# Attention preparation hosted in the feed-forward block ahead of it and in the score loop, with fp32r shift turns, on one Trainium2 core

## The chip, the cores and the metric

The kernel runs on one core of one Trainium2 (trn2) chip. The metric is the device time of one execution in microseconds (us), lower is better. TensorE (PE) multiplies, VectorE (DVE), ScalarE (ACT) and GpSimd (POOL) work on tiles, and SyncE (SP) issues most DMAs.

## What is computed

The reference carries x, 4 x 256 tokens of 256 features, through six residual stages. The change touches the borders of the fifth, an attention with ALiBi bias and low-rank keys and values:

```python
x = x + 0.5 * _L0_ffn_ref(_layernorm(x), ...)      # dense plus 2 of 8 experts, GELU
x = x + _L0_attn_ref(_layernorm(x), ...)
x = x + 0.5 * _L0_ffn_ref(_layernorm(x), ...)
x = x + 0.5 * _L1_ffn_ref(_layernorm(x), ...)      # 4 of 8 experts, ReLU
x = x + _L1_attn_ref(_layernorm(x), ...)
x = x + 0.5 * _L1_ffn_ref(_layernorm(x), ...)

# _L1_attn_ref, 16 heads of 16
c_kv = hidden_states @ w_dkv.T                     # 128 columns
q = (hidden_states @ w_q.T).reshape(B, S, HEADS, HEAD_DIM)
k = (c_kv @ w_uk.T).reshape(B, S, HEADS, HEAD_DIM)
v = (c_kv @ w_uv.T).reshape(B, S, HEADS, HEAD_DIM)
scores = jnp.einsum('bqhd,bkhd->bhqk', q, k) * scale + alibi_bias(S)[None, None]
attn = jax.nn.softmax(scores, axis=-1)
out = jnp.einsum('bhqk,bkhd->bqhd', attn, v).reshape(B, S, HIDDEN)
return out @ w_o.T
```

## The kernel before

The 1024 tokens are two blocks of 512 (`BLK`), and every stage goes over both, block 0 and then block 1. Each engine has its own program, written out by hand; semaphores tie them. Matrices are multiplied as three fp32r products: a value is split into a high part (rounded by ScalarE, names ending in `_hi`) and a low part (value minus high part, by VectorE or GpSimd, `_lo`), and `split3` (lines 578 to 581) issues high by high, high by low and low by high.

**The block ahead.** The ReLU feed-forward (`ffn1`) has 8 units, one per expert. Unit n: upper half (lines 731 to 734, into PSUM bank n % 3), relu twice on ScalarE (lines 1118, 1119), low part on GpSimd (line 523), lower half (`down1`, line 740) two units later (`LAG`), and the accumulate into x on VectorE (`acc1`, line 1579). The routing chain (logits, top 4, exponentials by ScalarE in `exps`, weights) must end before unit 0 is accumulated, and `down1` of unit n waits for the accumulate of unit n - 2. Its block 1 also carries the rounding of the attention weights (`wa_h` on ScalarE at unit 2, `wa_l` in four pieces on GpSimd at units 4 to 7), the constant rows of the key stacks (unit 4), and the statistics and normalisation of the attention's block 0 (units 4 and 5, `prepare_at`).

**The attention.** `attn1` on TensorE (line 753) turns z of block 0 (in `block_start`), finishes the last two units, and then projects c, q in two halves of 8 heads and k in two halves for block 0, turns z of block 1, projects v in two halves, and c and the first half of q of block 1. SyncE writes each half of q and k, high and low parts, to DRAM (`write`) and reads them back stacked by head (`read`: three DMAs into `qs`, six into `ks`), 96 rows of 32 that make the three products one. Four stack parts of 8 heads are in SBUF at a time.

**The loop.** 78 steps, one per head (64 heads) and a tail. At step s: `scores(s)`; at step s >= 7 `scores_t(s - 7)`, the turned scores whose exponential ScalarE takes; every fourth step a `shift_turn`, and from step 14 on every fourth a `pv`. VectorE adds the bias to each score and keeps the row minimum (`bias_min`, line 1662), which `shift_hi` and `shift_lo` split into columns of `shift`. `shift_turn` (line 862) turns four 128-column tiles of `shift` through `pe.transpose` with the f32 identity, and ScalarE copies the result to rows 96 to 127 of the query stack. The missing projections of block 1 (k half 0, q half 1, k half 1) stand at steps 1, 3 and 5:

```python
for s in range(4 * HEADS + SUM):
    if s < 4 * HEADS:
        scores(s)
    if s == 1:
        project_k(1, 0)
    if s == 3:
        project_q(1, 1)
    if s == 5:
        project_k(1, 1)
    if TURN <= s < 4 * HEADS + TURN:
        scores_t(s - TURN)
```

## Time and profile before

| | |
|---|---|
| median of 3 runs | 534.08 us (532.31 to 534.1) |
| the profiled execution's own time | 532.84 us |
| its span in the profile | 531.1 us |
| mean granted TensorE clock | 0.982 of 2.4 GHz |
| busy: PE, DVE, ACT, POOL | 497.2, 384.8, 252.4, 109.6 us |

The span is what the profile shows of one execution; the execution's own time has a little around it. In the profile PE is the matrix products, PEld their weight loads, which run beside them. A product's record begins when it starts and ends when its result is out, so that records overlap: the distance between two starts is what one costs. A line number is that of the kernel before. `x8` behind a row says that it merges eight instructions, and the bracket gives the idle time before it and who ended it.

### The profile page before, as it was taken

The numbers are of one execution on the slowest core, as the hardware profiler recorded it, in microseconds if no ns is written. First come the engines' busy times: TensorE is split into PE (matmuls) and PEld (weight loads), VectorE is DVE, ScalarE is ACT, GpSimd is POOL, SyncE is SP. The second block draws the span as 40 slices with busy tenths as digits, with TensorE's granted clock in tenths as the row PEclk, the third lists the DMA queues.
The fourth block names the chain that finished last, engine by engine and source line by source line (L and its number), as shares of the span: only waits on it lengthen the run. The fifth ranks groups of instructions, "written<-read, shape, count | busy, mean of one in ns | idle before, by whom it ended". The sixth has DMA issues, their size and how long they took to land.

```text
span 531.1 us, 9082 instructions
## 1 busy us (share of the span) xinstructions
PE 497.2 (94%) x3074; PEld 422.9 (80%) x3074; DVE 384.8 (72%) x1196; ACT 252.4 (48%) x539; POOL 109.6 (21%) x170
## 2 busy tenths in 40 slices
PE   2999999999999999999999997899789989799996
PEld 1788888888888888888888886788667878678885
DVE  4669787674687674688588787878767878648776
ACT  3657643525323525324574237456445766644441
POOL 1001000110010110010002005637403333414352
PEclk9999999999999999999999999899997999899999
DMA  6432320000000000001200000276488430000011
GB/s 206 118 90 68 97 56 1 1 1 1 2 0 1 1 1 1 1 1 41 60 21 0 2 1 2 91 81 118 150 187 269 111 79 3 1 2 1 3 38 41
DMA packets 18797, 25.87 MB, mean 49 GB/s; under 512 B 2848, under 2 KB 12832, under 8 KB 18752
## 3 DMA queue, kind: packets, MB, share of 16 engines
q1 hardware_dynamic: 17696, 24.78, 17.8%
q10 hardware_dynamic: 1056, 0.51, 0.3%
q8 instruction: 25, 0.41, 0.3%
q14 instruction: 20, 0.16, 0.1%
HBM read 17.42 MB, written 5.24 MB: 43 GB/s over the span
## 4 chain that ended last, share of the span: by engine, by line
PE 79%; DVE 9%; issue 4%; ACT 3%; POOL 2%; SPq 2%; DMA 1%; DVEq 0%; ACTq 0%; POOLq 0%
PE ps L579 22%; PE ps L581 21%; PE ps L580 21%; DVE x L1590 3%; PE ps L908 2%; PE ps L860 2%; PE ps L594 2%; PE ps L891 2%; PE ps L981 1%; DVE ps L1673 1%; POOL al L523 1%; PE ps L872 1%; PE ps L889 1%; ACT z L1013 1%; PE ps L970 1%
## 5 line engine op out<-in xcount | busy, mean ns | idle before, releaser
L579 PE MATMUL ps<-zh,w0u_h 128*128 128x512 f32 x256 | 103.1, 403 | 1.5 <-ACT zh L1020 1.5
L581 PE MATMUL ps<-zl,w0u_h 128*128 128x512 f32 x256 | 102.3, 400 | 0.0
L580 PE MATMUL ps<-zh,w0u_l 128*128 128x512 f32 x256 | 102.1, 399 | 0.0
L1042 ACT ACTIVATE gel<-ps 128x512 f32<-128x512 f32 x64 | 38.2, 597 | 104.4 <-PE ps L581 104.3
L1408 DVE TENSOR_TENSOR act<-gel,ps 128x512 f32<-128x512 f32 x64 | 43.7, 683 | 42.4 <-ACT gel L1042 42.2
L579 PE MATMUL ps<-w0d_h,ah 128*128 128x256 f32 x256 | 73.0, 285 | 0.4
L581 PE MATMUL ps<-w0d_l,ah 128*128 128x256 f32 x256 | 71.5, 279 | 0.0
L580 PE MATMUL ps<-w0d_h,al 128*128 128x256 f32 x256 | 71.4, 279 | 0.0
L1048 ACT ACTIVATE ah<-act 128x512 fp32r<-128x512 f32 x64 | 40.2, 629 | 40.3 <-DVE act L1408 40.3
L1590 DVE SCALAR_TENSOR_TENSOR x<-ps,aff,x 128x256 f32<-128x256 f32 x128 | 53.0, 476 | 8.9 <-PE ps L581 7.1
L579 PEld LDWEIGHTS ps<-zh,w0u_h 128*128 128x128 f32 x256 | 48.7, 190 | 12.8 <-ACT zh L1020 1.8
L523 POOL TENSOR_TENSOR al<-act,ah 128x512 fp32r<-128x512 f32 x32 | 42.0, 1313 | 79.1 <-ACT ah L1119 75.8
L1415 DVE TENSOR_TENSOR al<-act,ah 128x512 fp32r<-128x512 f32 x64 | 43.8, 684 | 19.9 <-ACT ah L1048 19.6
L581 PEld LDWEIGHTS ps<-zl,w0u_h 128*128 128x128 f32 x256 | 48.6, 190 | 11.8
L580 PEld LDWEIGHTS ps<-zh,w0u_l 128*128 128x128 f32 x256 | 48.7, 190 | 9.6
L579 PEld LDWEIGHTS ps<-w0d_h,ah 128*128 128x128 f32 x256 | 48.0, 188 | 3.7 <-issue 1.4
L580 PEld LDWEIGHTS ps<-w0d_h,al 128*128 128x128 f32 x256 | 48.0, 188 | 2.2
L1673 DVE CUSTOM_DVE_ANT_0 ps<-ps,bias 128x256 f32<-128x256 f32 (+1 forms) x128 | 42.5, 384 | 9.1 <-PE ps L860 8.3
L581 PEld LDWEIGHTS ps<-w0d_l,ah 128*128 128x128 f32 x256 | 48.0, 188 | 0.0
L1390 DVE SCALAR_TENSOR_TENSOR macc<-ps,aff,macc 128x256 f32<-128x256 f32 x112 | 46.3, 475 | 0.4
L579 PE MATMUL ps<-w_h,ah 128*128 128x256 f32 x128 | 36.8, 287 | 3.8 <-DVE x L1590 3.4
L500 POOL TENSOR_SCALAR ssq_e<-ssq 128x4 f32<-128x4 f32 x12 | 2.3, 193 | 184.4 <-ACT sq L1027 184.3
(182 smaller groups left out, 1039.7 us busy)
## 6 DMA issues: line engine op xcount, KB each, us to landing
stage<-in_w_dram SPq DMA_DIRECT2D x16, 384.0 KB, 3.0
qs<-split_out SPq DMA_DIRECT2D x24, 128.0 KB, 3.0
ks<-split_out SPq DMA_DIRECT2D x48, 64.0 KB, 2.9
stage<-in_w_dram SPq DMA_DIRECT2D x8, 256.0 KB, 2.7
ks<-pad SPq DMA_DIRECT2D x6, 256.0 KB, 9.7
ks<-pad SPq DMA_DIRECT2D x1, 1024.0 KB, 8.8
split_out<-qh SPq DMA_DIRECT2D x4, 256.0 KB, 2.6
split_out<-ql SPq DMA_DIRECT2D x4, 256.0 KB, 3.0
```

The lines of the kernel that those rows point to most:

```text
L523: nc.gpsimd.tensor_tensor(al[:, slot, :], act32[:, n % 2, :], ah[:, slot, :].bitcast(F32), ALU.subtract).then_inc(al1_s, 1)
L579: pe.matmul(o, lh, rh, start=start, stop=False, **kw)
L580: pe.matmul(o, ll, rh, start=False, stop=False, **kw)
L581: return pe.matmul(o, lh, rl, start=False, stop=stop, **kw)
L594: mm = pe.transpose(ps[:, kc, t * P:(t + 1) * P], z2[:, NORMS[p][1], t, kc * P:(kc + 1) * P], ident[:, :])
L1042: nc.scalar.activation(gel[:, n % 2, :], ps[:, 2 * (n % 2), :], ACT.Gelu_apprx_tanh).then_inc(gelu_s, 1)
L1048: nc.scalar.activation(ah[:, n % NA, :], act32[:, n % 2, :], ACT.Copy).then_inc(ah_s, 1)
L1390: i = V.scalar_tensor_tensor(sums[:, t, :], o, a, sums[:, t, :], ALU.mult, ALU.add)
L1408: V.tensor_tensor(act32[:, n % 2, :], gel[:, n % 2, :], ps[:, 2 * (n % 2) + 1, :], ALU.mult)\
L1415: V.tensor_tensor(al[:, n % NA, :], act32[:, n % 2, :], ah[:, n % NA, :].bitcast(F32), ALU.subtract)\
L1590: i = V.scalar_tensor_tensor(xt, ps[:, base + t // 2, (t % 2) * D:(t % 2 + 1) * D], aff[:, b, t, e:e + 1], xt, ALU.mult, ALU.add)
L1673: i = V.tensor_tensor_reduce(s, s, bias[:, cols], 1.0, FAR, ALU.add, ALU.min, nmin[:, hd // GROUP % 2, c, j:j + 1])
```

## The change

It moves preparation, and it changes how the shift columns are turned.

- **Block 0** of the attention is prepared inside block 1 of the feed-forward ahead of it, which it calls the host (`hosts_attn1`). VectorE takes the statistics at unit 1 ahead of the routing, GpSimd scales there, ScalarE normalises at unit 2. TensorE turns z after the upper half of unit 4, and projects c at unit 5, q at units 5 and 6, k at units 6 and 7. The attention weights are rounded at unit 0 (low parts at units 0 to 3), the constant rows at unit 1. Their loads start when the last lower half of the GELU feed-forward is done. The upper halves of the host go through two PSUM banks instead of three, and z and k of block 0 are split into unused slots of the query stack (`zh2`, `zl2`, `kh[0]`, `kl[0]`).
- **Block 1** is prepared in the loop: v half 1 of block 0 at step 1, z turned at step 8, c and q half 0 at step 11, k half 0 at 14, q half 1 at 17, k half 1 at 20, with ScalarE's and VectorE's parts one step later. The banks and the waits that guard them follow.
- **The queue** reads the first stack before it writes k half 1.
- **The shift columns** of the four tiles of a turn lie 32 columns apart in `pad`, so that the tiles overlap, and a turn is four plain fp32r products with an identity that ScalarE has rounded.

```diff
...
 Z_STEP = 66
+V0_STEP = 1
+Z1_STEP, C1_STEP, K10_STEP, Q11_STEP, K11_STEP = 8, 11, 14, 17, 20
...
         ql = sb("ql", [P, 2, BLK], F32R)
-        kh, kl = ah, al
...
         ks = sb("ks", [P, SLOTS, 2, SEQ], F32R)
+        zh2, zl2 = [qs[:, i:i + 4, :].rearrange("p (c s) q -> p c (s q)", c=KC) for i in (0, 4)]
+        kh, kl = [[qs[:, i:i + 4, :].rearrange("p (m s) q -> p m (s q)", m=2), t] for i, t in ((8, ah), (12, al))]
...
         pbt = sb("pbt", [P, 2, 4, 3 * P])
-        shift = macc[:, :, :].rearrange("p t d -> p (t d)").rearrange("p (s c m) -> p s c m", s=2, c=4)
...
+        ident_r = wr_h[:, 0, 0, :]
+        shift = pad[:, 0:2 * (K_ROWS + P)].rearrange("p (s m) -> p s m", s=2)
+        shift_cols = shift[:, :, K_ROWS:K_ROWS + P].rearrange("p s (c m) -> p s c m", c=4)
...
+        def hosts_attn1(st, b):
+            return st.kind == "ffn1" and st.after == "attn1" and b == 1
...
-            return 5 if b == 0 else 4
+            return 1 if hosts_attn1(st, b) else 5 if b == 0 else 4
...
+        def up_bank(n):
...
+            return n % 2 if "attn1" in stages and n // U1 == blocks_before_attn1 - 1 else n % 3
...
+        def zt_bank(p, kc):
...
+            return {attn1_p: (2, 3), attn1_p + 1: (PV_BANK, OUT_BANK)}.get(p, (0, 1))[kc]
...
+        def split_z(p):
+            return (zh2, zl2) if p == attn1_p else (zh, zl)
...
             if "attn1" in stages:
-                for b in range(2):
-                    sp.wait_ge(x_s[b], last_ffn0 + 1)
+                sp.wait_ge(down_s, U0 * f0)
...
                 sp.wait_ge(zero_s, 6 * 16)
-                for m, kind in ((0, 0), (1, 0), (0, 1), (1, 1)):
+                for m, kind in ((0, 0), (0, 1), (1, 0)):
                     write(0, m, kind)
-                for h in range(4):
+                read(0)
+                write(0, 1, 1)
+                for h in range(1, 4):
...
                         ln_scale(norm(st, b) + 1)
-                    if st.k + b == 1 and c >= U1 - WL and "attn1" in stages:
-                        i = c - (U1 - WL)
+                    if hosts_attn1(st, b) and c < WL:
+                        i = c
...
                     nc.gpsimd.memset(va[:, :, :, HD:HD + 1], 1.0).then_inc(wal_s, 1)
-                    nc.gpsimd.memset(shift[:, :, :, :], 0.0).then_inc(shz_s, 1)
+                    pool.wait_ge(zero_s, 6 * 16)
+                    pool.wait_ge(pad_s, 16)
+                    nc.gpsimd.memset(shift.bitcast(F32), 0.0).then_inc(shz_s, 1)
                     pool.wait_ge(shz_s, 1)
-                    nc.gpsimd.memset(shift[:, :, :, ONE_COL:ONE_COL + 1], 1.0).then_inc(shz_s, 1)
+                    nc.gpsimd.memset(shift_cols[:, :, :, ONE_COL - K_ROWS:ONE_COL - K_ROWS + 1].bitcast(F32), 1.0).then_inc(shz_s, 1)
...
                         if n >= 3:
-                            pe.wait_ge(ah1_s, n - 2)
+                            pe.wait_ge(ah1_s, n - 1 if hosts_attn1(st, b) else n - 2)
                         for kc in range(KC):
-                            mm = split3(ps[:, n % 3, :], w1_h[:, c, kc * P:(kc + 1) * P], w1_l[:, c, kc * P:(kc + 1) * P],
+                            mm = split3(ps[:, up_bank(n), :], w1_h[:, c, kc * P:(kc + 1) * P], w1_l[:, c, kc * P:(kc + 1) * P],
...
                             logits(3, routed["ffn1", fb])
+                        host = hosts_attn1(st, b)
+                        if host and c == 4:
+                            transposes(attn1_p)
+                        if host and c == 5:
+                            pe.wait_ge(wal_s, WL)
+                            split_ready(attn1_p)
+                            project_c(0)
+                        if host and c == 6:
+                            project_k(0, 0)
+                        if host and c == 7:
+                            project_k(0, 1)
...
                             down1(n - LAG)
+                        if host and c == 5:
+                            project_q(0, 0)
+                        if host and c == 6:
+                            project_q(0, 1)
...
                 block_start(st, 0)
-                pe.wait_ge(wal_s, WL)
-                split_ready(p)
-                project_c(0)
-                project_q(0, 0)
-                project_q(0, 1)
-                project_k(0, 0)
+                project_v(0)
                 pe.wait_ge(acc_s, E * f0 + U1 * st.d1 - 1)
-                project_k(0, 1)
-                transposes(p + 1)
-                project_v(0)
-                project_v(1)
-                split_ready(p + 1)
-                project_c(1)
-                project_q(1, 0)
...
                         scores(s)
-                    if s == 1:
-                        project_k(1, 0)
-                    if s == 3:
-                        project_q(1, 1)
-                    if s == 5:
-                        project_k(1, 1)
...
                         project_v(2 + V_STEPS.index(s))
+                    if s == V0_STEP:
+                        project_v(1)
+                    if s == Z1_STEP:
+                        transposes(p + 1)
+                    if s == C1_STEP:
+                        split_ready(p + 1)
+                        project_c(1)
+                        project_q(1, 0)
+                    if s == K10_STEP:
+                        project_k(1, 0)
+                    if s == Q11_STEP:
+                        project_q(1, 1)
+                    if s == K11_STEP:
+                        project_k(1, 1)
...
                 if g == 0:
+                    pe.wait_ge(ident_r_s, 1)
                     pe.wait_ge(shz_s, 2)
-                    pe.wait_ge(ch_s, 2)
-                    pe.wait_ge(cl_s, 2)
+                    pe.wait_ge(v_s, 2)
...
                 for i in range(4):
-                    mm = pe.transpose(ps[:, 2, i * P:(i + 1) * P], shift[:, g % 2, i, :], ident[:, :])
+                    mm = pe.matmul(ps[:, 2, i * P:(i + 1) * P], shift[:, g % 2, SLOT * i:SLOT * i + P], ident_r,
+                                   start=True, stop=True)
...
                             logits_t_out(routed["ffn1", fb], 3)
+                        host = hosts_attn1(st, b)
+                        if host and c == 6:
+                            q_hi(0, 0)
+                        if host and c == 7:
+                            q_hi(0, 1)
...
                             act.wait_ge(ob_ps, 8)
-                        nc.scalar.activation(act32[:, n % 2, :], ps[:, n % 3, :], ACT.Relu)
-                        nc.scalar.activation(ah[:, (U0 * f0 + n) % NA, :], ps[:, n % 3, :], ACT.Relu).then_inc(ah1_s, 1)
+                        nc.scalar.activation(act32[:, n % 2, :], ps[:, up_bank(n), :], ACT.Relu)
+                        nc.scalar.activation(ah[:, (U0 * f0 + n) % NA, :], ps[:, up_bank(n), :], ACT.Relu).then_inc(ah1_s, 1)
+                        if host and c == 4:
+                            z_hi(attn1_p)
+                        if host and c == 5:
+                            c_hi(0)
+                        if host and c in (6, 7):
+                            k_hi(0, c - 6)
...
                             normalise(p + b + 1)
-                        if fb == 1 and c == 2 and "attn1" in stages:
+                        if host and c == 0:
...
                             nc.scalar.activation(wa_h[:, :], wa_raw, ACT.Copy).then_inc(wah_s, 1)
-                        if fb == 1 and c == 4 and "attn1" in stages:
+                        if host and c == 1:
...
                             nc.scalar.activation(pad[K_ROWS:P, :], rows_raw, ACT.Copy).then_inc(rows_s, 1)
+                            nc.scalar.activation(ident_r, ident[:, :], ACT.Copy).then_inc(ident_r_s, 1)
...
                 p = st.p
-                z_hi(p)
-                c_hi(0)
-                q_hi(0, 0)
-                q_hi(0, 1)
-                k_hi(0, 0)
-                k_hi(0, 1)
-                normalise(p + 1)
-                z_hi(p + 1)
                 v_out(0)
-                v_out(1)
-                c_hi(1)
-                q_hi(1, 0)
-                k_hi(1, 0)
-                q_hi(1, 1)
-                k_hi(1, 1)
...
                                 out_hi(n, t)
+                    if s == Z1_STEP - 4:
+                        normalise(p + 1)
...
                         normalise(p + 2)
+                    if s == V0_STEP + 1:
+                        v_out(1)
+                    if s == Z1_STEP + 1:
+                        z_hi(p + 1)
+                    if s == C1_STEP + 1:
+                        c_hi(1)
+                        q_hi(1, 0)
+                    if s == K10_STEP + 1:
+                        k_hi(1, 0)
+                    if s == Q11_STEP + 1:
+                        q_hi(1, 1)
+                    if s == K11_STEP + 1:
+                        k_hi(1, 1)
...
                                 out_lo(3, 1)
+                        host = hosts_attn1(st, b)
...
                             left_acc(st, b, 2 - c)
+                        if host and c == 1:
+                            prepare(attn1_p, 0)
...
                             acc1(n - 3)
+                        if host and c == 4:
+                            z_lo(attn1_p)
+                        if host and c == 5:
+                            c_lo(0)
+                        if host and c in (6, 7):
+                            q_lo(0, c - 6)
+                            k_lo(0, c - 6)
...
                         first = prepare_at(st, b)
-                        if c == first or c == first + 1:
+                        if not host and c in (first, first + 1):
...
                 dve.wait_ge(kh_s, 2 * b + m + 1)
-                if b:
-                    dve.wait_ge(written_s[1][m], 32)
-                V.tensor_tensor(kl[:, m, :], ps[:, k_bank(b, m), :], kh[:, m, :].bitcast(F32), ALU.subtract)\
+                V.tensor_tensor(kl[b][:, m, :], ps[:, k_bank(b, m), :], kh[b][:, m, :].bitcast(F32), ALU.subtract)\
...
                 left_acc(st, 0, 3)
-                z_lo(p)
...
                 prepare(p + 1, 0)
-                c_lo(0)
-                q_lo(0, 0)
-                q_lo(0, 1)
-                k_lo(0, 0)
-                k_lo(0, 1)
-                z_lo(p + 1)
-                c_lo(1)
-                q_lo(1, 0)
...
                         bias_min(s)
-                    if s == 1:
-                        k_lo(1, 0)
...
                         shift_lo(s // GROUP)
-                    if s == 3:
+                    if s == Z1_STEP + 1:
+                        z_lo(p + 1)
+                    if s == C1_STEP + 1:
+                        c_lo(1)
+                        q_lo(1, 0)
+                    if s == K10_STEP + 1:
+                        k_lo(1, 0)
+                    if s == Q11_STEP + 1:
                         q_lo(1, 1)
-                    if s == 5:
+                    if s == K11_STEP + 1:
```

The places in the programs of the engines, as built:

ScalarE in block 1 of the host, from the copy of unit 0's logits (`small`, before) and from the relu of unit 0 (after), to the exponentials of the routing (`lex`). Before:

```order
L1032 ACTIVATE small<-ps 8x512
L1118 ACTIVATE act<-ps 128x512
L1119 ACTIVATE ah<-ps 128x512
L1118 ACTIVATE act<-ps 128x512
L1119 ACTIVATE ah<-ps 128x512
L1118 ACTIVATE act<-ps 128x512
L1119 ACTIVATE ah<-ps 128x512
L1036 ACTIVATE lex<-lsh 128x32
L1130 ACTIVATE wa_h<-va 128x1792
```

and now:

```order
L1158 ACTIVATE act<-ps 128x512
L1159 ACTIVATE ah<-ps 128x512
L1176 ACTIVATE wa_h<-va 128x1792
L1158 ACTIVATE act<-ps 128x512
L1159 ACTIVATE ah<-ps 128x512
L1179 ACTIVATE pad<-pbt 32x512
L1180 ACTIVATE wr_h<-ident 128x128
L1158 ACTIVATE act<-ps 128x512
L1159 ACTIVATE ah<-ps 128x512
L1071 ACTIVATE lex<-lsh 128x32
L1048 ACTIVATE z<-x,shift_z,zs 128x256 x4
```

The weights, the constant rows (`pad`) and the identity (into `wr_h`) stand ahead of `lex`, and the normalisation (`z`) right behind it, ahead of unit 3's relu.

TensorE in the loop, steps 9 to 11 and the scores of step 12. `ks,qs` with 256 columns alone are scores, `qs,ks` pairs are turned scores, `wr_h,pad` is a shift turn, `zh` and `zl` with `wa` are c and q. There was nothing of block 1 at these steps before. Now:

```order
L910 MATMUL ps<-wr_h,pad 128x128 x4
L895 MATMUL ps<-ks,qs 128x256
L898 MATMUL ps<-ks,qs 128x256
L924 MATMUL ps<-qs,ks 128x128
L926 MATMUL ps<-qs,ks 128x256
L898 MATMUL ps<-ks,qs 128x256
L924 MATMUL ps<-qs,ks 128x128
L926 MATMUL ps<-qs,ks 128x256
L603 MATMUL ps<-zh,wa_h 128x512
L604 MATMUL ps<-zh,wa_l 128x512
L605 MATMUL ps<-zl,wa_h 128x512
L603 MATMUL ps<-zh,wa_h 128x512
```

Eight more of the `wa` products follow before the next score.

The SP queue around the first stack read. Before:

```order
L401 DMA split_out<-qh 128x512
L401 DMA split_out<-ql 128x512
L401 DMA split_out<-qh 128x512
L401 DMA split_out<-ql 128x512
L401 DMA split_out<-ah 128x512
L401 DMA split_out<-al 128x512
L401 DMA split_out<-ah 128x512
L401 DMA split_out<-al 128x512
L412 DMA qs<-split_out 32x4x256 x3
L420 DMA ks<-split_out 16x4x256 x6
```

and now:

```order
L422 DMA split_out<-qh 128x512
L422 DMA split_out<-ql 128x512
L422 DMA split_out<-qs 128x512 x2
L422 DMA split_out<-qh 128x512
L422 DMA split_out<-ql 128x512
L433 DMA qs<-split_out 32x4x256 x3
L441 DMA ks<-split_out 16x4x256 x6
L422 DMA split_out<-qs 128x512 x2
```

The last pair of writes, k half 1 (`qs`, where its parts now lie), stands behind the first read.

## Rows read from the trace of the kernel before

**Rows 1.** The page, part 1: busy us (share of the span) xinstructions of each engine.

```profile
PE 497.2 (94%) x3074; PEld 422.9 (80%) x3074; DVE 384.8 (72%) x1196; ACT 252.4 (48%) x539; POOL 109.6 (21%) x170
```

**Rows 2.** Busy time by stretch: us, PE, PEld, DVE, ACT, POOL, PEclk, DMA share, GB/s.

```profile
373.40:390.50 17.10, 13.00 (x59) 10.36 (x57) 9.45 (x24) 8.53 (x15) 4.23 (x8) 0.90 0.60 184
390.50:405.20 14.70, 12.81 (x63) 10.74 (x63) 13.08 (x69) 6.47 (x13) 2.43 (x6) 0.82 0.78 202
405.20:450.00 44.80, 42.36 (x419) 34.27 (x419) 36.62 (x204) 30.67 (x70) 16.94 (x42) 0.98 0.36 100
```

**Rows 3.** The same view, one stretch of 2 us.

```profile
402.00:404.00 2.00, 2.00 (x11) 2.00 (x11) 1.64 (x10) 0.98 (x2) 0.87 (x3) 0.50 0.84 255
```

**Rows 4.** Waits of TensorE, 373 to 412 us: total, times, longest.

```profile
PE ps L594 <- ACT z L1013: 2.6, 1, 2.6
```

**Rows 5.** Timeline of TensorE, feed-forward block 1: start, us, line, operation.

```profile
360.98 0.39 PE L579 MATMUL ps<-zh,w_h 128*128 128x512 f32 x1
...
362.34 0.28 PE L579 MATMUL ps<-w_h,ah 128*128 128x256 f32 x1
...
363.75 0.40 PE L579 MATMUL ps<-zh,w_h 128*128 128x512 f32 x1
```

**Rows 6.** Timeline of VectorE, the same block.

```profile
352.12 0.19 DVE L1328 COPY lg<-ps 128x32 f32<-128x32 f32 x1 [2.33 <-PE ps L609]
...
357.67 3.42 DVE L1590 SCALAR_TENSOR_TENSOR x<-ps,aff,x 128x256 f32<-128x256 f32 x8
```

**Rows 7.** Timeline of ScalarE, the same block.

```profile
354.70 0.23 ACT L1036 ACTIVATE lex<-lsh 128x32 f32<-128x32 f32 x1
354.82 1.71 ACT L1130 ACTIVATE wa_h<-va 128x1792 fp32r<-128x1792 f32 x1
...
364.78 2.08 ACT L1013 ACTIVATE z<-x,shift_z,zs 128x256 f32<-128x256 f32 x4 [1.15 <-POOL shift_z L496]
```

**Rows 8.** Timeline of GpSimd, the same block.

```profile
362.90 0.19 POOL L486 TENSOR_SCALAR zs_e<-mv 128x4 f32<-128x4 f32 x1 [1.08 <-DVE mv L1296]
...
364.70 1.16 POOL L537 TENSOR_TENSOR wa_l<-va,wa_h 128x448 fp32r<-128x448 f32 x1
365.81 1.30 POOL L523 TENSOR_TENSOR al<-act,ah 128x512 fp32r<-128x512 f32 x1
```

**Rows 9.** Timeline of the SP queue, first stack read.

```profile
383.46 1.85 SPq L412 DMA_DIRECT2D qs<-split_out  x3
385.35 2.77 SPq L420 DMA_DIRECT2D ks<-split_out  x6
```

**Rows 10.** Timeline of TensorE, first score, turned score and PV.

```profile
390.50 0.39 PE L857 MATMUL ps<-ks,qs 96*128 96x256 f32 x1 [0.84 <-DMA ks<-split_out]
...
397.17 0.28 PE L889 MATMUL ps<-qs,ks 128*128 128x128 f32 x1
...
405.24 1.08 PE L908 MATMUL ps<-pbt,va 128*32 128x256 f32 x8
```

**Rows 11.** Timeline of VectorE, steps 4 to 8 of the loop.

```profile
394.93 0.69 DVE L1603 SCALAR_TENSOR_TENSOR ql<-ps,qh 128x512 fp32r<-128x512 f32 x1
395.53 0.29 DVE L1673 CUSTOM_DVE_ANT_0 ps<-ps,bias 128x128 f32<-128x128 f32 x1
...
399.24 0.29 DVE L1673 CUSTOM_DVE_ANT_0 ps<-ps,bias 128x128 f32<-128x128 f32 x1
```

**Rows 12.** Timeline of TensorE, a shift turn and what follows.

```profile
415.05 0.60 PE L872 MATMUL ps<-ident,macc 128*128 128x128 f32 x4
415.40 0.36 PE L579 MATMUL ps<-wa_h,ch 128*128 128x256 f32 x1
415.61 0.28 PE L580 MATMUL ps<-wa_h,cl 128*128 128x256 f32 x1
```

**Rows 13.** Timeline of TensorE, an fp32r product of 128 columns.

```profile
407.37 0.22 PE L889 MATMUL ps<-qs,ks 128*128 128x128 f32 x1
407.44 0.33 PE L891 MATMUL ps<-qs,ks 128*128 128x256 f32 x1
```

88 lines of the change are left out of this document (44 added, 44 removed).

## Prediction

> **What bounds the kernel now.** I read the page first: TensorE is busy for 94% of the span of 531.1 us, 497.2 us [rows 1]. So a gain must come from the few places where it waits or runs at a low clock, or from its own work. Then I cut the span into stretches. From 345 us to 373.4 us, the feed-forward block ahead of the attention, TensorE is hardly idle. The projections from there to the first score take 17.1 us at a mean clock of 0.90; the first fourteen steps of the loop take 14.7 us at 0.82; after them TensorE is busy for 42.36 of 44.80 us [rows 2]. In the two slow stretches the clock stands either at 1.00 or at 0.50, that is at 1.2 of 2.4 GHz [rows 3]. The waits say why: TensorE stood 2.6 us for ScalarE's normalised block 1 [rows 4], and its first score began 0.84 us late on a stack read [rows 10]. In the fourteen steps VectorE is busy for 13.08 of 14.70 us [rows 2]: there it is the bound, and TensorE starves beside it. After 405.2 us it is TensorE again.
>
> **The unit prices.** At the full clock the upper half of an expert, six products of 512 columns, takes 1.4 us of TensorE, and the lower half, twelve of 256 columns, takes 1.4 us [rows 5]. By these, c, each half of q, and the two halves of k together are 1.4 us each, one half of k and a v half are 0.7 us. A block's eight turns of z take 0.8 us if I take the 0.09 us per turn that four f32 turns show (0.35 us, 415.05 to 415.40) [rows 12].
>
> **Part A, to the first score.** Block 0's z turns, c, q and k go between units 4 to 7 of the block before. TensorE's work is the same wherever it stands: c, q, k are 5.6 us, and v half 0 is 0.7 us, so 6.3 us of the old stretch remain ahead of the first score. Block 1's turns, c and q half (3.6 us at full clock) and v half 1 (0.7 us) go behind it, and so does the 2.6 us wait. To the 6.3 us come stalls:
> - ScalarE now rounds the attention weights (1.71 us) after unit 0, and the constant rows and the identity (about 0.9 us) after unit 1; all of it stood behind the exponentials of the routing before. They started at 354.70 us [rows 7] and now start at 356.2 us by my walk. VectorE's routing weights wait for them, so the first accumulate slides from 357.67 us [rows 6] to 358.8 us, and TensorE's unit-2 lower half from 359.5 to 360.6 us. The new z turns fill 0.8 us of that; 0.65 us stay idle.
> - VectorE's statistics (1.8 us) move ahead of the routing. They fit in the 2.33 us in which it waited for the logits [rows 6], so I charge nothing; with that cover gone, each us would fall on the same chain.
> - GpSimd's four pieces of the weights' low part (1.16 us each) now alternate with units 0 to 3, with the 1.80 us of the scale between (362.90 to 364.70), and each unit's own low part takes 1.30 us [rows 8]. That is 11.6 us against 11.2 us of TensorE's four units. ScalarE's normalise (2.08 us) [rows 7] stands ahead of unit 3's relu. GpSimd's fourth piece ends at 363.7 us, 0.4 us after TensorE wants it.
> - The last three accumulates queue behind q's and k's low parts on VectorE: 0.6 us.
> - The stack. The SP queue must write q half 0, k half 0 and q half 1, then read: 1.85 us and 2.77 us of issue [rows 9], and 2.4 us from the end of issue (388.12) to the first score (390.50) [rows 10]. q half 1 is split at 374.3 us by my walk, its write is issued at 375.3 us, so the stack is there at 382.4 us; TensorE is ready at about 380.7 us. I take 1.9 us of waiting. The queue's order puts k half 1 behind this read; otherwise it would be 1 us more.
> Two stalls in that block, 0.6 us, are overtaken. So A takes 6.3 + 0.65 + 0.4 + 0.6 + 1.9 - 0.6 = 9.2 us instead of 17.1 us: **7.9 us gained**. Bounds: no new stall, 6.3 us; every stall twice as long, 12.8 us.
>
> **Part B, steps 0 to 14.** Before, 14.7 us, of which 6.7 us to the first turned score (390.50 to 397.17) and 8.1 us to the first PV (405.24) [rows 10]. VectorE needs 3.7 us for four heads (395.53 to 399.24), among it one low part like the one of 0.69 us at 394.93 [rows 11], so 3.0 us without: 0.75 us per step. In steps 0 to 7 nothing of block 1 is left to do but v half 1. I take 5.8 us, less than before by the 0.9 us of low parts that are gone. Steps 7 to 14 are 5.25 us of VectorE; z's, c's and q's low parts are 2.8 us more, and TensorE has 3.6 us (turns, c, q half) that it does in one piece while scores wait. The two do not overlap well, since c waits for z's low part behind two heads: 9.5 us. TensorE starves from 380.7 to 388 us, longer than ahead of the slow clock of before, so I add 2.0 us for half clock. B is then 17.3 us: **2.6 us lost**. Bounds: 14.0 us (VectorE's 10.5 + 2.8 us and a start of 0.7 us, no half clock) and 20.5 us.
>
> **Part C, from step 14.** k half 0, q half 1 and k half 1, once in steps 1 to 5, now stand at steps 14, 17 and 20 where TensorE is the bound: 2.8 us lost. The half clock that ran on to 407 us is over by then: 0.8 us gained. The shift turns: four f32 turns take 0.35 us, and the product behind them takes 0.21 us (415.40 to 415.61) where 256 columns go in 0.12 us: 0.44 us in all [rows 12]. An fp32r product of 128 columns is followed after 0.07 us [rows 13], so four are 0.27 us: 0.17 us less for each of 16 turns, 2.7 us, of which I take **2.0 us** because some lie where TensorE waits anyway. Bounds 0 and 2.7 us. Part C sums to zero. The rounding of the identity has no row: between the 0.23 us of the exponentials [rows 7] and the 1.71 us of the weights; 0.3 us is in the list above. The later clearing of the shift columns on GpSimd ends before the first turn. The earlier weight load moves to a time in which the DMA engines do nothing.
>
> The Trainium skill speaks against the turn: "TensorE: Matmul & The Clock Gate", Terms, says of transpose mode that it is 4x faster for FP32, and the new turn gives that mode up. By it a turn would cost four times as much; an fp32r product of 128 columns runs in 0.07 us without the mode [rows 13], so for this type the trace disagrees, and the sum goes by the row.
>
> **Sum.** 7.9 - 2.6 + 0 = 5.3 us. Against the profiled execution's own 532.84 us that gives **527.5 us**. The median of the three runs is 534.08 us, 1.2 us above it, and the lowest 532.31 us; 0.5% (2.7 us) is about what a measurement of this kernel can tell from no change.
>
> **Rivals.**
> - *The fill hides it all.* Block 1's split runs in VectorE's gaps and the clock stays up, so B takes 14.0 us: 524.2 us. For it: VectorE is idle while TensorE does c and q in one piece. Against: TensorE starves from 380.7 us on, and both drops of the clock in this region came behind such a time.
> - *The host block eats it.* The upper halves go through two PSUM banks there instead of three: unit n now needs the relu of unit n - 2, which sits behind weights, rows and normalise on ScalarE. If the late exponentials, the weights' low part and the stack cost 5 us more than I have, it comes to 532.5 us, no change. For it: ScalarE's row of 1.71 us lands on a chain that TensorE already waited for.
> - *Slower: five stations.* Each preparation step of block 1 (z, c with q, k, q, k) makes TensorE wait for a split on ScalarE and VectorE: 0.5 us of high part (1.71 us for 1792 columns [rows 7], here 512), 0.69 us of low part [rows 11] and a head of 0.75 us ahead of it, 1.9 us in all. It decides if three steps (2.6 us of loop) are less than that round trip with its queues. Stalling in full at all five is 9.5 us, where I have 1.5 us in B: 8 us more, 535.5 us.
> - *Slower: the turn loses its mode.* Four times 0.35 us is 1.40 us, 1.13 us above the 0.27 us that I have, for 16 turns 18 us: 545.5 us. The products of 0.07 us [rows 13] speak against it. This is what the Trainium skill's rule named above would make of the turn.
> - *The turns are not on the path.* Then the 2.0 us are missing: 529.5 us.
>
> **How the numbers follow.** The forecast 0.42, the hidden fill 0.27, turns off the path 0.05, the host block 0.16, five stations 0.08, the lost mode 0.02. The first three are faster by over 0.5%, and some of the host block's cases too: 0.76; within 0.5% 0.14; slower 0.10. The range runs from 521.5 us (the hidden fill with half of A's stalls gone) to 532.5 us (the host block); what is left out are the two slower cases, 0.10, and some 0.1 of the others' tails.
>
> **What would show it.** The first score at about 382.5 us, behind a wait for the stack of some 2 us; the first PV near 400 us; the clock at 0.50 for some 4 us behind the first score. The exponentials of the second block near 356 us. A turn of four products followed after 0.27 us. If the first score comes later than 386 us, part A is wrong; if the waits for VectorE's low parts in steps 9 to 20 sum to over 4 us, the stations are right; if the clock stays at 1.00, the hidden fill is.

## The result, and the profile after

The changed kernel is slower: a median of 536.58 us (12 runs, 533.61 to 537.72) beside 532.33 us (12 runs, 530.2 to 534.12) for the kernel before on the same chip. The ratio is 1.0068, its interval 1.005 to 1.0086. The forecast was 527.5 us. The profiled execution took 536.63 us, with a span of 534.9 us, against 532.84 and 531.1 us before: 3.8 us more, which is what has to be explained.

The page's part 1, after:

```profile
PE 498.6 (93%) x3074; PEld 425.1 (79%) x3074; DVE 386.2 (72%) x1196; ACT 251.6 (47%) x540; POOL 109.4 (20%) x170
```

Against [rows 1] TensorE has 1.4 us more of work and 2.4 us more of idle time. Where they lie shows when the attention is cut at its first score, its first PV product and its last. The timeline of TensorE, first score, the c product of block 1 and the first PV (start, us, line, operation, idle before and what ended it):

```profile
382.24 0.35 PE L895 MATMUL ps<-ks,qs 96*128 96x256 f32 x1 [1.52 <-DMA ks<-split_out]
...
396.40 0.52 PE L603 MATMUL ps<-zh,wa_h 128*128 128x512 f32 x1 [1.30 <-ACT zh L1055]
396.72 0.63 PE L604 MATMUL ps<-zh,wa_l 128*128 128x512 f32 x1
397.15 0.63 PE L605 MATMUL ps<-zl,wa_h 128*128 128x512 f32 x1
...
403.46 0.64 PE L943 MATMUL ps<-pbt,va 128*32 128x256 f32 x8 [0.71 <-DVE cl L1666]
```

The view of busy time, cut at those points (columns as in [rows 2]):

```profile
373.40:382.24 8.84, 6.78 (x50) 6.13 (x49) 6.68 (x17) 2.32 (x5) 3.76 (x5) 1.00 0.86 229
382.24:403.46 21.22, 16.64 (x78) 14.24 (x79) 13.73 (x72) 9.00 (x18) 4.06 (x10) 0.76 0.43 116
403.46:475.00 71.54, 64.04 (x597) 51.80 (x597) 50.69 (x266) 45.95 (x104) 25.04 (x62) 0.95 0.25 75
```

| stretch | before, us | after, us | lost | forecast |
|---|---|---|---|---|
| 373.4 us to the first score | 17.1 | 8.84 | -8.3 | -7.9 |
| first score to first PV | 14.7 | 21.2 | +6.5 | +2.6 |
| first PV to last PV | 66.0 (405.24 to 471.2) | 71.5 (403.46 to 475.0) | +5.5 | 0 |

Behind the last PV both need 59.9 us more. So the host block gave what the forecast said, and 14 steps and the rest of the loop took 12.0 us where the forecast had 2.6 us.

Who stood still there is seen in VectorE's waits, 380 to 425 us (line, waited for: total, times, longest):

```profile
DVE ps L1725 <- PE ps L898: 8.1, 7, 3.3
DVE zl L1364 <- ACT zh L1055: 2.3, 1, 2.3
DVE al L1670 <- ACT ah L1194: 1.7, 2, 1.4
```

VectorE, the bound of the first steps, stands 2.3 us for the rounded z and 1.4 us for the last half of k. The timelines of ScalarE and VectorE show why:

```profile
390.29 0.49 ACT L1256 ACTIVATE pbt<-ps 128x384 f32<-128x384 f32 x1 [0.36 <-PE ps L926]
393.39 0.59 ACT L1249 ACTIVATE qs<-ps 32x512 fp32r<-32x512 f32 x1 [2.60 <-PE ps L910]
394.00 0.49 ACT L1256 ACTIVATE pbt<-ps 128x384 f32<-128x384 f32 x1
394.39 1.08 ACT L1055 ACTIVATE zh<-ps 128x512 fp32r<-128x512 f32 x2
```

```profile
392.56 0.14 DVE L1725 DVE_READ_ACCUMULATOR2_ANT nmin<- 128x1 f32 x1
395.01 1.29 DVE L1364 TENSOR_TENSOR zl<-ps,zh 128x512 fp32r<-128x512 f32 x2 [2.31 <-ACT zh L1055]
...
401.27 0.30 DVE L1725 CUSTOM_DVE_ANT_0 ps<-ps,bias 128x128 f32<-128x128 f32 x1 [3.29 <-PE ps L898]
```

TensorE turned z at step 8 (from 390.06 us). But ScalarE's program has z's high part at step 9, behind that step's copy of the shift rows (L1249), and the copy waits 2.60 us for a shift turn that TensorE does in step 9 too. A turn falls on every fourth step, at 9 and again at 21, and the high part of k half 1 is placed at step 21: the same knot twice. VectorE, which runs in order, cannot pass its own wait; then TensorE has no scores, starts c 1.30 us late, and VectorE in turn waits 3.29 us for TensorE.

The Trainium skill, "TensorE: Matmul & The Clock Gate", Part 1, "Architectural detail: the array is 16× 32×32, not 1× 128×128", says of ScalarE and VectorE that they are strict first-in first-out; by that rule a free z in PSUM is of no use while the copy ahead of it waits, and the trace agrees: 2.60 us.

The clock is the second half of it. Busy time of stretches, after:

```profile
384.00:386.00 2.00, 0.62 (x3) 0.41 (x3) 2.00 (x13) 0.49 (x2) 1.43 (x3) 1.00 0.47 133
394.00:396.00 2.00, 0.48 (x3) 0.30 (x2) 0.99 (x2) 2.00 (x5) 0.49 (x2) 1.00 0.53 161
462.00:464.00 2.00, 0.40 (x4) 0.23 (x3) 1.01 (x6) 2.00 (x6) 0.19 (x1) 1.00 0.00 0
384.00:400.00 16.00, 12.35 (x48) 10.56 (x49) 10.07 (x54) 6.64 (x14) 3.46 (x8) 0.68 0.46 125
416.00:420.00 4.00, 3.20 (x16) 3.20 (x17) 2.36 (x14) 1.34 (x3) 0.82 (x2) 0.65 0.88 261
464.00:468.00 4.00, 3.82 (x24) 3.19 (x28) 0.85 (x2) 2.58 (x7) 1.45 (x4) 0.62 0.02 4
```

The first three rows are times in which TensorE starves, busy for 0.40 to 0.62 of 2.00 us; from 416 to 417 us it is busy for 0.20 of 1.00 us. Behind each of the four the granted clock stood at 0.50, that is 1.2 of 2.4 GHz, for some 3 to 6 us. The products of c above follow each other after 0.43 us, where at the full clock it is 0.23 us [rows 5].

### The profile page after: what moved, and what is told of

It reads as the page before. It is cut to its first block, busy times and chain, and to the rows that moved or that the text cites. A ratio compares the mean times of both kernels' runs of the same rounds, so it can differ in the third digit from the quotient of the medians.

```text
span 534.9 us, 9080 instructions
## 1 busy us (share of the span) xinstructions
PE 498.6 (93%) x3074; PEld 425.1 (79%) x3074; DVE 386.2 (72%) x1196; ACT 251.6 (47%) x540; POOL 109.4 (20%) x170
## 4 chain that ended last, share of the span: by engine, by line
PE 80%; DVE 7%; issue 4%; ACT 4%; POOL 3%; DMA 1%; SPq 0%; DVEq 0%; POOLq 0%; ACTq 0%
PE ps L603 23%; PE ps L605 22%; PE ps L604 22%; DVE x L1648 2%; PE ps L615 2%; PE ps L943 2%; POOL al L545 2%; PE ps L1016 1%; PE ps L898 1%; DVE ps L1725 1%; PE ps L926 1%; ACT z L1048 1%; PE ps L910 1%; PE ps L1005 1%; DMA x<-in_x_dram 1%
## 5 line engine op out<-in xcount | busy, mean ns | idle before, releaser
L605 PE MATMUL ps<-w0d_l,ah 128*128 128x256 f32 x256 | 71.5, 279 | 0.0
L1256 ACT ACTIVATE pbt<-ps 128x384 f32<-128x384 f32 x64 | 30.8, 494 | 19.8 <-PE ps L926 19.0
```

The lines of the kernel that those rows point to most:

```text
L605: return pe.matmul(o, lh, rl, start=False, stop=stop, **kw)
L1256: nc.scalar.activation(pbt[:, hd // GROUP % 2, hd % GROUP, :], ps[:, turned_bank(hd), 0:3 * P], ACT.Exp, scale=-1.0).then_inc(exp_s, 1)
```

## The experiments

Theory 1 (the place): two high parts stand behind a copy that waits for TensorE in the same step, and cost VectorE 2.3 + 1.4 us and the clock behind them. Theory 2 (the clock): starvation behind the first score costs on its own. Theory 3 (the turn): the fp32r turn costs as much as the f32 one, so that its 2.0 us are missing. Theory 4 (the split of the work): the move into the loop costs more than the host block gives. A rival to theory 1, "rival 3" below, says that every preparation step costs a full round trip wherever it stands.

Beside each median stands its ratio to the kernel before, run on the same chip, with its interval; it weighs all runs of both, so that it is not quite the ratio of the two medians. "Stages" are first score to first PV, and first PV to last PV, of the profiled execution, one for each kernel; after has 21.2 and 71.5.

**Steps 7 and 21 in place of 8 and 20**, so that no high part falls on a turn's step.

```
-    Z1_STEP, ..., K11_STEP = 8, 11, 14, 17, 20
+    Z1_STEP, ..., K11_STEP = 7, 11, 14, 17, 21
```

> The change with two constants moved: z of block 1 is turned at step 7 instead of 8 and k half 1 projected at step 21 instead of 20, so that ScalarE's high parts (one step later) no longer stand at a step whose number leaves 1 when divided by 4, where ScalarE first waits for the shift turn. Theory 1 (VectorE stands in order behind a high part that stands behind the shift turn): the waits of VectorE of 2.3 us for zh and 1.4 us for k's high part shrink to under 1 us each, and the time falls by 2 to 4 us against the change, to 533 to 535 us where the kernel before has 532. Theory 2 (the low clock behind the thin first steps is the cost): under 1 us of change. Rival 3 (any station costs a full round trip wherever it stands): no change within 1 us.

531.72 us (10 runs), ratio 0.999 (0.9955 to 1.0024): 5 us less than the change. Stages 20.0 and 67.9. VectorE's waits for the high parts of z and k, 2.3 and 1.7 us before, are 0.4 and 0.6 us: theory 1 holds for the waits, and rival 3 does not. Where the 5 us lie is less clear. The first stage is shorter by 1.2 us only, the second by 3.6 us, and in the second this execution has neither of the two falls of the clock that after has at 416 and 464 us.

**The turn in f32 again**, all else of the change kept.

```
-    mm = pe.matmul(..., shift[...], ident_r, start=True, stop=True)
+    mm = pe.transpose(..., shift[...].bitcast(F32), ident[:, :])
```

> The change with its shift turn made again as four f32 transposes with the f32 identity, all else as in the change. The trace of the change shows 0.39 us from the first product of a turn to the next instruction, where the f32 transposes before had 0.35 us and 0.08 us of delay behind them. Theory 3 (the fp32r turn costs as much as the f32 one): within 0.8 us of the change, and 0.35 us again from the turn to the next instruction. My forecast's price (0.27 against 0.44 us): 2 to 2.7 us slower than the change.

536.55 us (8 runs), ratio 1.0063 (1.0027 to 1.0099), as the change (1.0068). The turn neither causes the loss nor gives the 2.0 us of the forecast. Stages 20.7 and 68.4, but of an execution of 532.51 us, the shortest of the eight. It has both misplaced high parts (VectorE waits 1.8 us for z and 1.4 us for k half 1), and yet its clock stays up in the second stage. Busy time of four stretches, the last two as above:

```profile
415.00:416.00 1.00, 0.19 (x1) 0.19 (x2) 0.93 (x6) 0.28 (x1) 0.41 (x1) 1.00 0.64 240
460.00:462.00 2.00, 0.48 (x3) 0.34 (x3) 0.90 (x5) 2.00 (x7) 0.49 (x2) 1.00 0.00 0
416.00:420.00 4.00, 3.87 (x40) 3.17 (x39) 3.16 (x19) 2.57 (x6) 0.82 (x2) 1.00 0.86 243
464.00:468.00 4.00, 3.45 (x36) 2.56 (x28) 0.75 (x3) 2.51 (x8) 1.20 (x3) 1.00 0.02 4
```

TensorE starves as it does after, 0.19 of 1.00 us and 0.48 of 2.00 us, and the clock does not fall. So a starved time can be followed by the half clock and need not be, and 3.1 us of the second stage (71.5 against 68.4) go with that difference and not with the order of the work.

**Idle products** behind the scores of steps 1 to 6, two each, into a bank that nobody reads there.

```
+    if s == 1:
+        pe.wait_ge(acc_s, E * f0 + U1 * blocks_before_attn1)
+    if 1 <= s < TURN:
+        for _ in range(2):
+            pe.matmul(ps[:, 4, :], wa_h[:, 0:P], ch[:, :], start=True, stop=True)
```

> The change with two idle products of 512 columns into bank 4 after each of the scores 1 to 6; nothing reads them. They fill TensorE where it waits for VectorE. Theory 2 (low clock): the granted clock stays at 1.00 from 382 to 396 us instead of 0.50 for some 6 us, the first PV comes 2 to 3 us earlier and the time falls by 2 to 3 us. Theory 1 (order of ScalarE and VectorE at the stations): the clock rises but the time changes by under 1 us, since the waits for high parts remain.

534.54 us (10 runs), ratio 1.0025 (1.0002 to 1.0047). Stages 17.8 and 71.6. Busy time of the stretches from 384, 416 and 464 us:

```profile
384.00:400.00 16.00, 13.48 (x84) 11.24 (x83) 12.07 (x68) 7.83 (x16) 3.84 (x10) 1.00 0.60 140
416.00:420.00 4.00, 4.00 (x33) 3.24 (x32) 1.66 (x10) 2.23 (x5) 0.81 (x2) 0.68 0.73 195
464.00:468.00 4.00, 4.00 (x36) 3.01 (x36) 0.42 (x1) 1.14 (x4) 0.81 (x2) 0.71 0.00 0
```

The clock stays at 1.00 through the first steps, and the first stage is 3.4 us shorter with the waits for z (1.8 us) and k (1.4 us) still there. The clock has a price of its own.

**Only the host block**: block 0 hosted as in the change, block 1 prepared where it was before.

```
-    Z1_STEP, ..., K10_STEP, Q11_STEP, K11_STEP = 8, 11, 14, 17, 20
+    Z1_STEP, ..., K10_STEP, Q11_STEP, K11_STEP = 8, 11, 1, 3, 5
...
+    transposes(p + 1)
+    split_ready(p + 1)
+    project_c(1)
+    project_q(1, 0)
```

> Block 0 hosted in the feed-forward as in the change, but v half 1, z, c and q half 0 of block 1 stand ahead of the loop again and k half 0, q half 1, k half 1 at steps 1, 3 and 5, as before. It undoes the second half of the change. If the loop's stations are what costs (theories 1 and 2), it is faster than the change. The first score then waits for block 1's z: the last accumulate ended at 381.7 us in the change and z was ready at 387.7 us, so turns, splits, c and q half end near 393 us and the first score comes there, 2.5 us later than before (390.5 us). I expect 1 to 4 us slower than the kernel before, near the change. If hosting by itself pays, it is faster than the kernel before.

546.64 us (4 runs), ratio 1.0276 (1.0213 to 1.0338), some 14 us slower than before where 1 to 4 us were expected. TensorE's waits, 375 to 425 us:

```profile
PE ps L615 <- ACT z L1045: 6.4, 1, 6.4
PE ps L603 <- DVE ql L1651: 1.9, 2, 1.2
PE ps L603 <- ACT zh L1052: 1.5, 1, 1.5
PE ps L603 <- DVE al L1660: 0.9, 1, 0.9
```

With block 0 gone from there, nothing covers the residual, norm and rounding of block 1: the first score comes at 395.80 us, later than before (390.50). The clock adds to it: 0.54 from 386 to 396 us and 0.57 from 404 to 424 us. The move into the loop is what lets the hosting pay.

**Steps and idle products together.** The first and third edit.

> The change with both edits that helped: z turned at step 7 and k half 1 projected at step 21, and two idle products of 512 columns after each of the scores 1 to 6. The steps alone gave a ratio of 0.999 to the kernel before (5 us against the change), the idle products alone 1.0025 (2.3 us). If the order of the stations and the low clock are two separate costs, they add: 7 us against the change, 529 us, ratio 0.994. If they are the same 2 us seen twice (a station's stall that the low clock makes long), it is no faster than the steps alone, 531.5 us.

531.31 us (12 runs), ratio 0.9977 (0.9954 to 0.9999); 529 us were expected if the two gains add. Stages 18.6 and 67.9. In the profiled execution 3.0 us were lost ahead of the attention (first score at 385.28 us, see below). But behind the first score the gains do not add either: 146.5 us to the end of the span (531.8 - 385.28), against 147.8 us with the steps alone (530.0 - 382.20), where the sum of both gains would give 144.5 us. The clock stays up in the first steps and falls later, to 0.50 at 398 us.

**The kernel before with the fp32r turn alone.**

```
-    mm = pe.transpose(ps[...], shift[:, g % 2, i, :], ident[:, :])
+    mm = pe.matmul(ps[...], shift[:, g % 2, SLOT * i:SLOT * i + P], ident_r,
+                   start=True, stop=True)
...
+    nc.scalar.activation(ident_r, ident[:, :], ACT.Copy)
```

> The kernel before with the change's shift turn alone: columns in the padding tile, identity rounded by ScalarE, four plain fp32r products. Theory 3 (the fp32r turn costs what the f32 one costs): ratio 1.000 within 0.002. My forecast's price: 2 us faster, ratio 0.996.

534.43 us (12 runs), ratio 1.0038 (1.0013 to 1.0063): the turn does not make the old kernel faster; it is a little slower. Theory 3 had 1.000 within 0.002.

**ScalarE's order alone.** Steps 8 and 20 stay; in steps 9 and 21 the high part goes ahead of the copy and of the step's exponential.

```
+    if s == Z1_STEP + 1:
+        z_hi(p + 1)
+    if s == K11_STEP + 1:
+        k_hi(1, 1)
     (out_hi, shift_out, probs of the step)
...
-    if s == Z1_STEP + 1:
-        z_hi(p + 1)
...
-    if s == K11_STEP + 1:
-        k_hi(1, 1)
```

> The change with its steps (8 and 20) kept; only on ScalarE the high parts of z (step 9) and of k half 1 (step 21) stand ahead of that step's shift copy and exponential instead of behind them. Theory 1 in its narrow form (VectorE waits for a high part that stands behind the shift copy on ScalarE): the same gain as with the moved steps, 4 to 5 us against the change, 531 to 532.5 us. If instead the moved steps helped by their places on TensorE or by the clock, it stays at the change's 536 us.

532.81 us (12 runs, five of them near 528.6 and seven from 532.6 to 533.9), ratio 0.9975 (0.9944 to 1.0006), which lies wholly below that of the change. Stages 18.1 and 70.2. This is the narrowest test of theory 1: no step, product or transfer differs. ScalarE and VectorE at the same place:

```profile
391.61 0.60 ACT L1055 ACTIVATE zh<-ps 128x512 fp32r<-128x512 f32 x1 [0.36 <-PE ps L615]
392.46 0.60 ACT L1055 ACTIVATE zh<-ps 128x512 fp32r<-128x512 f32 x1 [0.25 <-PE ps L615]
393.85 0.59 ACT L1249 ACTIVATE qs<-ps 32x512 fp32r<-32x512 f32 x1 [0.79 <-PE ps L910]
```

```profile
393.02 1.28 DVE L1364 TENSOR_TENSOR zl<-ps,zh 128x512 fp32r<-128x512 f32 x2
```

The low part of z begins 2.0 us earlier (2.5 us counted from the first score, which came at 382.71 us), without a wait. Two lines moved give back 3.1 us of the first stage and 1.3 us of the second. The clock now stays up from 416 to 420 us, and falls at 459 us.

**Steps, idle products, and the constant rows and identity after unit 2** instead of unit 1 of the host block.

```
-    if host and c == 1:
+    if host and c == 2:
```

> As the kernel with moved steps and idle products, and the rounding of the constant rows and the identity on ScalarE stands at unit 2 behind the exponentials of the routing instead of at unit 1 ahead of them. The exponentials then start some 0.9 us earlier, and TensorE's 0.5 us ahead of the hosted z turns go. If that wait is on the path: 0.3 to 0.6 us less than with the other two edits. If the exponentials' delay is hidden: the same time.

533.49 us (12 runs), ratio 0.9994 (0.9971 to 1.0017). In the profiled execution the exponentials began at 354.85 us, 1.1 us earlier than after, but the first score came at 382.27 us, as after: TensorE now stood 0.9 us for the low part of the hosted z, a wait that after does not have. The median is no better than without this edit (531.31 us, 0.9977); the late exponentials cost nothing that these runs can tell.

**Only the loop**: ScalarE's order mended, nothing hosted, block 0 prepared in front of the loop.

```
-    return st.kind == "ffn1" and st.after == "attn1" and b == 1
+    return False
...
+    project_c(0)
+    project_q(0, 0)
+    project_q(0, 1)
+    project_k(0, 0)
+    project_k(0, 1)
```

> The other half of the change: block 0 is prepared ahead of the loop as before (three upper banks, weights rounded at units 2 and 4 to 7, nothing hosted), block 1 in the loop at steps 8 to 20, with ScalarE's high parts of z and k half 1 ahead of the shift copy. The first score waits for the first stack read, which I put near 388 us against 390.5 before and 382.2 in the change. The loop after it is that of the kernel with ScalarE's order alone. If hosting is worth its 6 us of earlier start: 537 to 539 us. If hosting only moves work that would fit elsewhere: 532 us.

538.13 us (6 runs), ratio 1.0123 (1.0087 to 1.0159). Its first score comes at 390.87 us, behind a wait of 7.28 us for the stack: block 1's work, which covered that wait before, is gone from there. Together with the run of only the host block it shows that neither half is worth having alone: 1.0276 and 1.0123 apart, 0.9975 together (with the order mended).

**Order and idle products.**

> ScalarE's order alone (ratio 0.9975) plus two idle products after each of the scores 1 to 6. If the low clock of steps 2 to 8 is a cost of its own: 1 to 2 us less than the order alone, ratio 0.995. If it only hides behind VectorE, which sets the pace there: the same as the order alone.

528.62 us (6 runs), ratio 0.993 (0.9906 to 0.9955): 0.7% faster than the kernel before, and faster than the change. Stages 16.3 and 68.7. Its page, and its clock where after stood at 0.68:

```profile
PE 494.5 (94%) x3086; PEld 421.5 (80%) x3086; DVE 385.7 (73%) x1196; ACT 251.8 (48%) x540; POOL 109.3 (21%) x170
```

```profile
384.00:400.00 16.00, 14.12 (x98) 11.49 (x97) 13.16 (x69) 9.98 (x20) 4.55 (x11) 1.00 0.59 134
```

TensorE does 12 products more than after and is busy for 4.1 us less.

**Order and the f32 turn.**

> ScalarE's order alone, with the shift turn as f32 transposes. In the kernel before, the fp32r turn alone gave 1.0038 (1.0013 to 1.0063) although turn and follower take 0.56 us in both traces; in the change the f32 turn gave 0.9995 of it. If the turn costs the same in both forms: within 1 us of the order alone (532.8 us). If the fp32r form does cost 1 to 2 us: 531 us.

530.26 us (10 runs), ratio 0.9945 (0.9925 to 0.9965), where the fp32r turn gave 0.9975; the intervals overlap, but it points the same way as the turn alone. Stages 18.3 and 68.3.

**Order, idle products, f32 turn, rows after unit 2.**

> All that could help in one: ScalarE's order, f32 shift turns, idle products after scores 1 to 6, constant rows and identity rounded at unit 2. If the gains add: 530 us, ratio 0.994, faster than both kernels. If the order is all that counts: 532 to 533 us, ratio 0.998.

529.87 us (12 runs), ratio 0.9951 (0.9929 to 0.9972): no better than order and idle products alone. Stages 16.3 and 68.6, the same too.

**Reading the stages instead of the medians.** From the first score to the end of the span after takes 152.7 us (534.9 - 382.24), the order alone 148.2 us (530.9 - 382.71), the idle products alone 149.4 us (532.8 - 383.36): 4.5 and 3.3 us less. Both together should be 144.9 us and are: 526.9 - 382.01. That it fits so well is partly luck. The first stage would be 14.7 us by such a sum and is 16.3 us: the two edits remove in part the same loss. The second would be 70.3 us and is 68.7 us, and there the three executions differ in the clock, which fell at 416 and 464 us with the idle products alone, from 459 to 465 us with the order alone, and only from about 457 to 460 us with both.

The last experiment has 144.8 us (531.1 - 386.33), though its span is 4.2 us longer. That was lost ahead of the attention, and the clock shows it. Busy time of two stretches, first of order and idle products, then of the last experiment:

```profile
328.00:336.00 8.00, 6.23 (x32) 5.68 (x33) 7.20 (x18) 3.75 (x12) 5.40 (x6) 0.79 0.00 1
340.00:352.00 12.00, 10.21 (x67) 8.99 (x68) 9.80 (x28) 6.48 (x12) 3.77 (x5) 1.00 0.37 43
```

```profile
328.00:336.00 8.00, 5.32 (x35) 4.95 (x36) 7.79 (x17) 3.76 (x12) 6.07 (x6) 1.00 0.00 1
340.00:352.00 12.00, 9.10 (x50) 8.62 (x51) 8.52 (x21) 4.23 (x8) 4.49 (x7) 0.72 0.27 33
```

In one execution the clock falls behind 330 us, after TensorE was busy for 0.23 of 2.00 us, in the other behind 342 us, after 0.50 of 2.00 us. ScalarE reaches the rows and the identity, which the last experiment rounds later, only behind 354 us; and the steps with the idle products, without that edit, have the same fall behind 342 us, a clock of 0.72 from 340 to 352 us, and TensorE busy for 0.01 of 2.00 us at 328 us before it without a fall. So it is not the edit: the same program goes either way there, and the first score comes 3 to 4 us later for it (385.28 and 386.33 against 382.01 us).

A third such place is 464 us: 0.62 after, 1.00 with the steps moved. It is there in after and in before (0.66 from 460 to 464 us), so it is no part of the 3.8 us; but the second stage of an execution that has it (after, the order alone, order and idle products, among others) is not to be compared with one that has not (the steps moved, the f32 turn, steps with idle products).

## Why the prediction was wrong

**Part A was right.** The first score came at 382.24 us (forecast 382.5), behind a stack wait of 1.52 us (forecast 1.9); the exponentials at 355.92 us (356.2); rounding the identity took 0.31 us (0.3); TensorE's stall ahead of the hosted z turns 0.5 us (0.65). The gain was 8.3 us where 7.9 had been worked out. It holds for executions in which the clock falls behind 330 us, as it did before; where it falls behind 342 us the first score comes at 385 to 386 us.

**Part B failed, at the sentence that c waits for z's low part behind two heads.** It priced steps 7 to 14 by VectorE's work and TensorE's in one piece, 9.5 us, and never read ScalarE's order at step 9. Measured, the stage was 21.2 us against 17.3, outside the upper bound of 20.5. With the order mended it is 18.1 us: the misplaced high part, taken alone, is worth 3.1 of the 3.9 us missed. The 2.0 us for half clock are right for that mended order, where keeping the clock at 1.00 saves 1.8 us (16.3 us); in the change it saves 3.4 us, so the two edits remove in part the same loss. The bare stage of 16.3 us is 1.0 us more than the 15.3 us that the forecast had without half clock. The first PV at "near 400 us" came at 403.46 us, and at 400.8 us with the order mended.

**Part C: two terms were wrong, and it is the larger miss, 5.5 us lost instead of 0.** The 2.0 us gain of the turns is missing (below). And k half 1 at step 20 was priced as TensorE's work alone, while its high part at step 21 stands behind a turn's copy: VectorE waits 1.4 us and TensorE then 1.06 us, behind which the clock was 0.65 from 416 to 420 us. What that wait costs without the clock can be seen in the f32 turn's execution: its stage of 68.4 us is 2.4 us over before, and only 0.5 us over the 67.9 us of the steps moved, which have neither the long wait nor a fall. The other 3.1 us of the 5.5 go with the falls at 416 and 464 us. The 2.8 us that k half 0, q half 1 and k half 1 cost late in the loop roughly fit (order with idle products has 68.7 us against 66.0 before, 2.7 us), but the 0.8 us that should have come back beside them do not show, and no run separates the two.

A gained 0.4 us more than forecast, B lost 3.9 us and C 5.5 us more; that gives 527.5 - 0.4 + 3.9 + 5.5 = 536.5 us, where the profiled execution took 536.63 us.

**The turn.** The rows, after:

```profile
401.66 0.56 PE L910 MATMUL ps<-wr_h,pad 128*128 128x128 f32 x4
402.05 0.33 PE L895 MATMUL ps<-ks,qs 96*128 96x256 f32 x1
402.22 0.29 PE L898 MATMUL ps<-ks,qs 96*128 96x256 f32 x1
```

Four products are followed after 0.39 us (not 0.27), and the score behind them after 0.17 us: 0.56 us in all, as with f32 in [rows 12]. What failed is the choice of the row: the 0.07 us of [rows 13] is a single product of 128 columns whose successor has 256. In a run of four each product has a weight load of its own. Four of them, after and before:

```profile
401.54 0.53 PEld L910 LDWEIGHTS ps<-wr_h,pad 128*128 128x128 f32 x4
414.95 0.46 PEld L872 LDWEIGHTS ps<-ident,macc 128*128 128x128 f32 x4
```

One load takes 0.19 us for fp32r and 0.14 us for the f32 transposes (medians of 64), so the four start about 0.11 us apart in both forms. That the loads space the products would fit this, but no run shows it. The lost mode, forecast at 18 us by the rival, cost nothing of that kind: four products are followed after 0.39 us, not 1.40 us.

The Trainium skill, "TensorE: Matmul & The Clock Gate", Back-to-back issue gap, says that in a stream of load and product pairs both set the spacing, and gives about 81 ns at 128 columns. Four would be 0.32 us by it, an estimate, where the trace has 0.39 us; the rule points the right way. With 0.32 us for 0.27 us the gain of a turn would have been 0.12 us instead of 0.17 us; the runs show none.

**The rivals.** Five stations, 535.5 us at a chance of 0.08, came nearest in time, but that is in part luck. Its test, waits for VectorE's low parts of over 4 us in steps 9 to 20, is not met: TensorE stood 1.3 us for z, 0.3 us for k half 0 and 0.7 us at the first PV, and VectorE's own waits for high parts in these steps are 3.2 us (4.5 us with the 1.4 us of step 21). Not every station stalls, only the two whose high part shares its step with a turn; c, q half 1 and k half 0 pass for 0.3 us each. The hidden fill is refuted by the clock, 0.68 from 384 to 400 us, and the host block by part A. The turns off the path had the 2.0 us missing, as they are, but for another reason: the turn did not get cheaper.

**What stays open.** The fp32r turn measured 1.0038 alone, and 0.9975 against 0.9945 with the order mended, both against it, but 1.0068 against 1.0063 in the change itself; its rows are equal within 0.01 us, and where the 1 to 2 us come from was not found. In the profiled execution with the turn alone 0.8 of the 1.4 us more lie ahead of the first score, where no turn is made: the queue needed 4.01 us to issue the six reads into `ks` (2.77 us before), and the first score waited 2.80 us for them. Nor was it found what makes the clock fall in one execution and not in another behind the same starved time, at 330 or at 342 us, at 416 us, and near 460 us.

## What to carry to other kernels

Before work is placed at a step of a hand-written order, write down for every engine what stands ahead of it in that very step, and ask of each of these instructions whether it waits for something done in the same step. A periodic instruction (here every fourth step) must be checked against every place, since 9 and 21 fall on it and 12, 15 and 18 do not. And where a bound engine starves TensorE behind a fresh start, a few products that nobody reads can be cheaper than the half clock that follows: here 12 of them gave back 3.3 us behind the first score. And of work that is to be moved, ask what it covers where it stands: block 1's work ahead of the loop hid the wait for the stack, and block 0's hid the normalisation of block 1.

## What was not expected of the hardware

- Four fp32r products of 128 columns with a weight load each take as long as four f32 transposes (0.56 us with the follower).
- The clock fell to 0.50 at five places of one execution (near 332, 386, 397, 417 and 465 us, after). The same starved time is not always followed by it: TensorE busy for 0.20 of 1.00 us from 416 us and the clock falls, 0.19 of 1.00 us from 415 us with the f32 turn and it stays at 1.00.
- This moves the whole time by up to 4 us, as much as the change itself: the twelve runs of the change took from 533.61 us at a mean clock of 0.985 to 537.72 us at 0.980.
